# A second set of source rows, scaled from the first one layer later, and a reordered load queue, in a four-layer graph network

## The chip, the cores and the metric

The kernel runs on one core of a Trainium2 chip. The metric is device time in microseconds (us) of one execution, lower is better. The core has five instruction queues that run side by side and meet only at semaphores: PE (matmul), DVE (vector), ACT (activation functions, here mostly "scale and shift one tile of rows"), POOL (here: indirect gathers and scatters) and SP (here: nothing but issuing DMAs). Each queue runs its instructions in the order in which they are written; an instruction that waits on a semaphore holds all that stand behind it in its own queue.

## The reference, cut to what matters

50,000 nodes with 128 features, 12,500 edges sorted by target. Four layers, numbered 0 to 3 as in the code, each with a layer norm over the features after it:

```python
x = layernorm(x + L0(x, edges))      # attention over incoming edges
x = layernorm(x + L1(x, edges))      # mean of the neighbours, two products, relu
x = layernorm(x + L2(x, edges))      # per relation (8) product, summed over incoming edges
x = layernorm(x + L3(x, edges))      # messages by edge type (3), update by node type (3)

# layernorm(x) = (x - mean) / sqrt(var + 1e-5)

def L2(h, weight, src, dst, rel):
    hw = einsum('ni,rio->nro', h, weight)
    return segment_sum(hw[src, rel], dst)
def L3(h, W_e, b_e, W_n, b_n, src, dst, etype, ntype):
    parts = [relu(h)]
    for t in range(3):
        msg = where(etype == t, relu(h[src] @ W_e[t].T + b_e[t]), 0)
        parts.append(segment_sum(msg, dst))
    agg = concatenate(parts)
    return where_by_type(ntype, [agg @ W_n[t].T + b_n[t] for t in range(3)]) + h
```

A node without incoming edges gets zero from layer 2. For such a node the layer norm after layer 2 is only a second layer norm of what layer 1 left.

## The kernel before

Two kinds of rows are worked on. A **dense block** is 500 nodes (125 partitions x 4); there are 100 of them, and each goes through the layers as if it had no edges. An **edge chunk** is 500 edges; there are 25, and each layer runs over all of them, with one dense block (two in layer 0) threaded through each round. The rows of the source and the target node of every edge are kept apart in DRAM, as `source_rows` (`s_rows[0..2]`, one for the input of layers 1 to 3) and `target_rows` (`d_rows[0..2]`). In each layer a chunk's source rows are loaded by SP, and POOL then overwrites those whose node has incoming edges with the node's updated row, gathered from `target_rows` at `slot_all`.

Layer 1 makes two sets of source rows at once. ACT normalizes `ys` (a row plus its update) with the factors of statistics group "first" into `so`, the rows for layer 2, and again with those of group "third" into `so3`, the rows for layer 3 of a node that layer 2 leaves alone. Both have the same mean; their variances differ by the two lines in `variances` (L740, L743). SP stores both in `store_sources1` (L349, L351).

A round of layer 2 (loop variable c) on each queue, in the order of the code:

- DVE: `scan` of chunk c (L807), five of the seven relation masks of chunk c+1 (`masks`, L937, one product of `rel == r` and the chunk's rows per relation), the dense block (`read`, `stats`), the chunk's target rows (L946), variances, the first two masks of chunk c+2 (`EARLY = 2`), and then `scales`, whose last instruction (L757) releases ACT by `s_ln`. `masks` waits for the relation numbers of its chunk (`rl`).
- ACT: after `s_ln` of round c two sets of dense rows (L1039), the turned rows (L1076), the source rows of chunk c+3 (`evacuate_sources`, L1105), L1082, the target rows into `do`, and the dense block's result into `res`. So ACT's round c runs beside DVE's round c+1.
- PE: turns of rows (L1575, L1312), the eight relation products of chunk c+1 (L1561) in two halves with the turn of chunk c+2 between them, and the dense products (L1318, L1323, L1383).
- POOL: four gathers for chunk c+3 (L528), three lookups of node types.
- SP, one list of DMAs per round: load a dense block (L236), the source rows of chunk c+4 (`sources2`, L398), the relation numbers of chunk c+2 (`relations2`, L403), target rows (L413), `same` (L420), then wait for `do` of round c-1 and store it (`store2`, L426), then store a dense result (L242).

Layer 3 starts when POOL has seen every store of layer 2's target rows land (`landed(3)`) and gathers its first chunk. SP issues seven pairs of its first loads (L467 to L485) before the last `store2`. Layer 1 starts the same way behind layer 0.

Of the kernel before, what the change touches and what calls it, by code (L numbers as in the profile page):

```python
# [13 lines left out]
D = 128  # L14
# [33 lines left out]
def gnn_kernel(nc, x, src, dst, srcP, dstP, nextP, eattrT, etype3, etype8, eweight, ntype3, ntypeP, Wq, Wk, Wv, We, gate,  # L48
# [25 lines left out]
    with ctx:  # L74
# [6 lines left out]
        def two(make, name, *a):  # L81
# [53 lines left out]
        rel = two(sb, "rel", [D, C], I32)  # L135
        run, run2 = sb("run", [D, 3, C + 1]), sb("run2", [D, 3, C + 1])
        masked = sb("masked", [D, REL, C])
        den = sb("den", [R, T * H])
        headsel = sb("headsel", [D, H])
# [34 lines left out]
        SINGLE = ("tS tD eS eD eL pA pB pR vA vE vL eX eR nS nD nF yb eN sc", "tS tD eS eD pR vA nS nD rd",  # L174
                  "tS eS pM pR vA vM nD nF", "tS tD eS eD pM pR vM vA eX vN nD rd bs xb")
        RINGS = ({"aux": 2, "g": 3, "stS": 2, "stD": 2},
# [7 lines left out]
        s_slot = [sem(f"layer1_slots_{i}") for i in range(EC - SOONER + 1)]  # L184
# [28 lines left out]
        def _(sp):  # L213
# [145 lines left out]
            store_sources0(EC - 1)  # L359
# [17 lines left out]
            for c in range(EC):  # L377
                d = block_of(1, c)
                load_dense(d + 3)
                if there(c + 3):  # L380
                    rows1(c + 3)
                if there(c + 2):
                    targets1(c + 2)
                    sums1(c + 2)
                if c >= 1:
                    store_sources1(c - 1)
                    store_targets1(c - 1)
                    store_dense(d - 7)
# [39 lines left out]
            sources2(0)  # L428
            relations2(0)
            sources2(1)  # L430
            relations2(1)
            sums2(0)
            targets2(0)
            sums2(1)
            sources2(2)
# [5 lines left out]
            stored(1)  # L441
            sources2(3)
            for c in range(EC):
                d = block_of(2, c)
                if d + 3 < NC:
                    load_dense(d + 3)
                if there(c + 4):
                    sources2(c + 4)
                if there(c + 2):
                    relations2(c + 2)  # L450
                if there(c + 1):
                    targets2(c + 1)
                if there(c + 2):
                    sums2(c + 2)
                if c >= 1:
                    store2(c - 1)
                store_dense(d - 7)

            def sources3(c):
                k, q = c % 3, ph[3]  # L460
                sp.wait_ge(q["tS"], at(c - 2))
                if c == 0:
                    sp.wait_ge(ph[1]["rd"], EC)
                elif c < 3:
                    sp.wait_ge(ph[2]["tS"], EC - 3 + c)
                for part in PARTS:
                    sp.dma_start(flat(xs3[k])[part, :], rows(s_rows[2])[c][part, :]).then_inc(q["ld"][k], 16)  # L467
# [10 lines left out]
            def sums3(c):  # L478
                b, q = c % 2, ph[3]
                sp.wait_ge(q["vA"], at((c - 1) * NT))  # L480
                if c < 2:
                    sp.wait_ge(ph[2]["vA"], EC - c)
                    sp.wait_ge(ph[2]["vM"], (EC - c) * (REL - 1))
                sp.dma_start(same[b][:, :], to_all(same_d, c)).then_inc(q["sm"][b], 16)
                sp.dma_start(rel[b][:, :], to_all(etype3, c)).then_inc(q["sm"][b], 16)  # L485
# [32 lines left out]
        def _(pool):  # L518
# [75 lines left out]

            def rows1(c):
                k, q = c % 4, ph[1]
                pool.wait_ge(s_slot[max(c + 1 - SOONER, 0)], 16 * T * (SOONER if c < SOONER else 1))
# [9 lines left out]
            for c in range(EC):  # L607
# [3 lines left out]
                if c % 3 == 0 and there(late):  # L611
                    slots1(late * T, (late + 1) * T, s_slot[1 + c // 3])
# [45 lines left out]
        def _(dve):  # L658
# [8 lines left out]
            for k in range(3):  # L667
                V.memset(bst[k][:, :, :], 0.0)
            V.memset(floors[:, 0:1], D * EPS * EPS)
# [242 lines left out]

            step(V.memset(run[:, 0, C:C + 1], 0.0))
            source_sums1(0)
            for c in range(EC - 1):
# [7 lines left out]
                scales(s, 6, s_ln)  # L923
            step(edge_rows1(EC - 1, TAIL, 0, 1, 2))
            variances(TAIL, 3, 1)
            scales(TAIL, 3, s_tail)
            for d in range(block_of(1, EC - 1), block_of(1, EC) + GAP):
# [50 lines left out]
            def message_sums(c):  # L978
# [4 lines left out]
                for t in range(NT):  # L983
                    dve.wait_ge(q["eX"], c * NT + (t + 1))
                    V.scalar_tensor_tensor(out=masked[:, t, :], in0=rel[b][:, :], scalar=float(t), in1=masked[:, t, :],
                                           op0=ALU.is_equal, op1=ALU.mult).then_inc(q["vM"], 1)
                for t in range(NT):
                    dve.wait_ge(q["vM"], c * NT + (t + 1))
                    scan(m, t, same[b][:, :], masked[:, t, :], ALU.mult, ALU.add,
# [42 lines left out]
        def _(act):  # L1032
# [157 lines left out]
            for c in range(EC - 1):  # L1190
# [12 lines left out]
                act.wait_ge(q["stS"][b], (c // 2) * 2 * ROWS)  # L1203
                normalize(so[b], ys[b], k % 2, 4)
                normalize(so3[b], ys[b], k % 2, 1).then_inc(q["nS"], 1)
# [12 lines left out]
            act.wait_ge(q["stS"][b], ((EC - 1) // 2) * 2 * ROWS)  # L1218
            normalize(so[b], ys[b], TAIL, 1)
            normalize(so3[b], ys[b], TAIL, 0).then_inc(q["nS"], 1)  # L1220
# [3 lines left out]

            evacuate_sources(0, 2, 7)
# [6 lines left out]
            for c in range(EC - 1):  # L1232
# [11 lines left out]
                evacuate_xt(d - 1)  # L1244
                act.wait_ge(q["stD"][b], (c // 2) * ROWS)
# [420 lines left out]
```

## Time and profile before

| | |
|---|---|
| median of 3 runs | 1717.78 us (1715.58 to 1718.99) |
| the profiled execution | 1722.77 us, of which its span is 1721.0 us |
| busy over the span | PE 81%, DVE 82%, ACT 65%, POOL 71% |
| layer 0, with start and end | about 0 to 670 us |
| layer 1 | about 670 to 970 us |
| layer 2 | about 970 to 1350 us |
| layer 3 | about 1350 to 1721 us |

The busy shares are means over four layers that have different limits; a single layer has to be read from its own stretch. Times in a trace row are us from the start of the span. An engine's row gives its start, its length, the engine, the line of the kernel, the operation, the tile written and the tile read, the shapes, the count of instructions that the row stands for, and in brackets the idle time before it with what ended it.

### The profile page before, as it was taken

What the parts mean: (1) busy time and instruction counts of PE and PEld (TensorE: products, weight loads), DVE (VectorE), ACT (ScalarE), POOL (GpSimd) and SP (SyncE); (2) the same over time, 40 slices, a digit from 0 to 9 for tenths busy, and PEclk for the clock granted to TensorE, in tenths of its full rate; (3) what the DMA queues carried; (4) which work ended last, traced back from release to release, by engine and by line L of the source; (5) the groups of instructions that cost most, each with busy time, mean ns of one, the idle gap of its engine ahead of it and who ended that gap; (6) DMA issues with size and microseconds to landing.
All of it is one profiled execution on the core that took longest, in us unless ns stands there. A gap on an engine that the chain in (4) does not pass through costs nothing.

```text
span 1721.0 us, 22842 instructions
## 1 busy us (share of the span) xinstructions
PE 1390.8 (81%) x6078; PEld 902.0 (52%) x6078; DVE 1410.1 (82%) x3005; ACT 1120.2 (65%) x2769; POOL 1230.3 (71%) x910
## 2 busy tenths in 40 slices
PE   4687777777777755787878589999998699999995
PEld 2454444544445434666666355555555355555552
DVE  4688888888888874998889679999998578877774
ACT  1567877778777783999999836666665344334442
POOL 7877777777788877778888387776330668888874
PEclk9678999999999987989999889999999899999998
DMA  7334444444434343677777535555543434333320
GB/s 169 85 68 101 112 98 98 105 104 112 99 98 108 82 130 73 187 201 192 197 196 194 161 87 144 150 141 137 148 119 94 99 94 101 99 94 93 98 74 22
DMA packets 165796, 205.06 MB, mean 119 GB/s; under 512 B 66825, under 2 KB 97920, under 8 KB 165668
## 3 DMA queue, kind: packets, MB, share of 16 engines
q1 hardware_dynamic: 108068, 179.45, 38.8%
q0 software_dynamic: 57600, 24.15, 8.0%
q8 instruction: 50, 0.82, 0.2%
q14 instruction: 78, 0.64, 0.2%
HBM read 147.12 MB, written 70.80 MB: 127 GB/s over the span
## 4 chain that ended last, share of the span: by engine, by line
PE 48%; DVE 16%; ACT 12%; issue 12%; POOL 9%; DMA 2%; SPq 1%; POOLq 0%; DVEq 0%; ACTq 0%
PE po L1323 22%; PE pt L1312 6%; POOL slot_all L528 6%; DVE masked L937 5%; DVE bst L732 4%; ACT x L1039 3%; PE pb L1329 2%; PE pb L1561 2%; PE po L1318 2%; PE po L1383 2%; PE pc L1431 2%; ACT so L1039 2%; PE pc L1312 2%; ACT do L1039 2%; ACT res L1039 1%
## 5 line engine op out<-in xcount | busy, mean ns | idle before, releaser
L528 POOL DMA_INDIRECT xs<-target_rows,slot_all x236 | 316.9, 1343 | 160.9 <-issue 68.8
L1039 ACT ACTIVATE x<-y,nmr,rst 125x128 f32<-125x128 f32 x800 | 322.3, 480 | 43.2 <-DVE nmr L757 43.2
L1323 PE MATMUL po<-wnt,rt 128*125 128x384 f32 x800 | 290.1, 508 | 0.0
L1312 PE MATMUL pt<-ident,x 125*128 125x125 f32 x800 | 134.6, 295 | 111.2 <-issue 82.3
L1323 PEld LDWEIGHTS po<-wnt,rt 128*125 128x125 f32 x800 | 158.3, 201 | 92.3 <-issue 14.4
L1323 PE MATMUL po<-wnt,run 128*125 128x384 f32 x600 | 201.5, 486 | 0.0
L535 POOL DMA_INDIRECT out_rows<-do,last_all x100 | 146.6, 1466 | 60.7 <-issue 40.0
L528 POOL DMA_INDIRECT xs<-in_x,src_all x100 | 133.8, 1338 | 53.7 <-issue 53.7
L1312 PEld LDWEIGHTS pt<-ident,x 125*128 125x128 f32 x800 | 100.1, 154 | 136.9 <-issue 100.9
L1039 ACT ACTIVATE do<-yd,nmr,rst 125x128 f32<-125x128 f32 x400 | 163.5, 482 | 6.2 <-DVE nmr L757 6.2
L1039 ACT ACTIVATE res<-sel,nmr,rst 125x128 f32<-125x128 f32 x400 | 163.5, 482 | 3.8 <-DVE nmr L757 2.6
L528 POOL DMA_INDIRECT slot_all<-slot_d,src_all x100 | 136.3, 1363 | 34.2 <-issue 33.9
L528 POOL DMA_INDIRECT ntd_all<-in_ntype,dst_all x100 | 138.2, 1382 | 30.5 <-issue 30.2
L535 POOL DMA_INDIRECT slot_d<-eid,last_all x100 | 134.6, 1346 | 30.5 <-issue 30.2
L1561 PE MATMUL pb<-masked,wr 128*128 128x500 f32 x350 | 155.8, 586 | 0.0
L732 DVE BATCH_NORM_STATS2 bst<-y 125x6 f32<-125x256 f32 x400 | 142.9, 419 | 3.8
L1323 PEld LDWEIGHTS po<-wnt,run 128*125 128x125 f32 x600 | 108.8, 188 | 68.3
L528 POOL DMA_INDIRECT xdb<-target_rows,slot_all x64 | 84.6, 1321 | 83.7 <-DMA target_rows<-do 61.1
L1318 PE MATMUL po<-ball,ones_bf 128*125 128x384 bf16 x412 | 97.5, 365 | 46.0 <-DVE sel L778 46.0
L1105 ACT ACTIVATE st<-pt 128x500 f32<-128x500 f32 x50 | 29.0, 579 | 148.4 <-PE pt L1312 148.4
L937 DVE SCALAR_TENSOR_TENSOR masked<-rel,st 128x500 f32<-128x500 int32 x175 | 106.8, 669 | 10.8 <-issue 4.3
L1383 PEld LDWEIGHTS po<-wab,xt 128*125 128x125 f32 x800 | 102.7, 190 | 20.0 <-issue 0.2
(186 smaller groups left out, 3024.5 us busy)
## 6 DMA issues: line engine op xcount, KB each, us to landing
xin<-in_x SPq DMA_DIRECT2D x100, 224.0 KB
out_rows<-res SPq DMA_DIRECT2D x100, 224.0 KB
same<-same_d SPq DMA_DIRECT2D x75, 250.0 KB, 4.1
source_rows<-so SPq DMA_DIRECT2D x75, 224.0 KB
target_rows<-do SPq DMA_DIRECT2D x75, 224.0 KB
xs<-source_rows SPq DMA_DIRECT2D x59, 224.0 KB
rel<-in_etype SPq DMA_DIRECT2D x50, 250.0 KB, 4.8
xd<-target_rows SPq DMA_DIRECT2D x46, 224.0 KB
```

Of the source, the lines that this page charges most:

```text
L528: return nc.gpsimd.indirect_dma_start(out=to, out_offset=None, in_=table, in_offset=bass.IndirectOffsetOnAxis(ap=index, axis=0), bounds_ch ...
L535: return nc.gpsimd.indirect_dma_start(out=table, out_offset=bass.IndirectOffsetOnAxis(ap=index, axis=0), in_=of, in_offset=None, bounds_ch ...
L732: last = V.bn_stats(to, y[:, j:j + 2, :].rearrange("p j d -> p d j"))
L937: V.scalar_tensor_tensor(out=masked[:, r, :], in0=rel[b][:, :], scalar=float(r), in1=st[:, :], op0=ALU.is_equal, op1=ALU.mult).then_inc(q[ ...
L1039: last = A(to[:, j, :], y[:, j, :], ACT.Identity, scale=rst[s][:, k:k + 1], bias=nmr[s][:, k:k + 1])
L1312: last = nc.tensor.transpose(tile_of(to, j), rows_[:, j, :], ident[0:R, 0:R])
L1318: mm(po[0:R, j * 512:j * 512 + NT * D], ones_bf[:, 0:R], ball[:, :, :].rearrange("k s d -> k (s d)"), start=True, stop=False, skip_group_c ...
L1323: last = mm(po[0:R, j * 512:j * 512 + NT * D], left(j), wnt[:, k, :, :].rearrange("k t d -> k (t d)"), start=start, stop=stop, skip_group_ ...
L1329: last = mm(to[0:R, j * D:(j + 1) * D], left(j), right, start=start and j == 0, stop=stop and j == T - 1, skip_group_check=True)
L1383: last = mm(po[0:R, j * 512 + NT * D:(j + 1) * 512], xt[:, j, :], wab[:, 0, :], start=False, stop=True, skip_group_check=True)
L1431: mm(pc[:, 0:C], ks[:, :], st[:, :], start=False, stop=False)
L1561: mm(pb[:, 0:C], wr[:, r, :], masked[:, r, :] if r else st[:, :], start=r == 0, stop=r == REL - 1).then_inc(q["pM"], 1)
```

## The change

`so3` and its store leave layer 1. DVE computes there one factor per row instead (`factors1`, two small instructions per chunk, kept in `again_all`). In layer 2 ACT multiplies the rows of `xs2` by that factor (`source_rows2`, four instructions per chunk), and SP stores them (`store_sources2`). `sources2` also waits for that read. Layer 3 uses buffers of its own for two inputs (`aux` for `same`, `rel3` for `rel`), so that its first loads need not wait for layer 2's masks. SP's order changes: the first loads of layers 2 and 3 move into the last round of the layer before, those of layer 1 ahead of three stores. The semaphores for late `slot_all` lookups become a ring of three.

```diff
@@ stored(p)
-                    if p < 2:
-                        sp.wait_ge(ph[p]["stS"][b], (1 + p) * ROWS * n)
+                    sp.wait_ge(ph[p]["stS"][b], ROWS * n)
                     sp.wait_ge(ph[p]["stD"][b], ROWS * n)
@@ store_sources1(c)
-                for part in PARTS:
-                    sp.dma_start(rows(s_rows[2])[c][part, :], flat(so3[b])[part, :]).then_inc(q["stS"][b], 16)
@@ SP, start of layer 1
-            store_sources0(EC - 1)
             ...
             rows1(1)
             sums1(1)
+            rows1(2)
+            targets1(1)
+            store_sources0(EC - 1)
             store_targets0(EC - 2)
-            rows1(2)
             store_targets0(EC - 1)
-            targets1(1)
@@ sources2(c)
                 sp.wait_ge(q["tS"], at(c - 2))
-                sp.wait_ge(o["stS"][c % 2], counted(c, 2 * ROWS))
+                sp.wait_ge(q["nS"], at(c - 2))
+                sp.wait_ge(o["stS"][c % 2], counted(c, ROWS))
@@ new on SP
+            def store_sources2(c):
+                b, q = c % 2, ph[2]
+                sp.wait_ge(q["nS"], c + 1)
+                for part in PARTS:
+                    sp.dma_start(rows(s_rows[2])[c][part, :], flat(so3[b])[part, :]).then_inc(q["stS"][b], 16)
@@ SP, layer 1's loop
                     sums1(c + 2)
+                if c == EC - 1:
+                    sources2(0)
+                    relations2(0)
+                    sources2(1)
+                    relations2(1)
+                    sums2(0)
+                    targets2(0)
+                    sums2(1)
+                    sources2(2)
                 if c >= 1:
                     store_sources1(c - 1)
...
             stored(1)
+            store_sources2(0)
             sources2(3)
+            store_sources2(1)
@@ SP, layer 2's loop
                 if there(c + 2):
                     sums2(c + 2)
+                if c == EC - 1:
+                    sources3(0)
+                    targets3(0)
+                    sums3(0)
+                    sources3(1)
+                    sums3(1)
+                    sources3(2)
                 if c >= 1:
                     store2(c - 1)
+                if there(c + 2):
+                    store_sources2(c + 2)
                 store_dense(d - 7)
...
-            sources3(0)
-            targets3(0)
-            sums3(0)
-            sources3(1)
             targets3(1)
-            sums3(1)
-            sources3(2)
             store2(EC - 1)
@@ new on DVE, called after scales in each round of layer 1
+            def factors1(c, s, third, first):
+
+                of = lambda a, g: a[s][:, g * T:(g + 1) * T]
+                step(V.scalar_tensor_tensor(out=of(tmp, 0), in0=of(ve, first), scalar=1.0 / D, in1=of(rst, first), op0=ALU.mult, op1=ALU.mult))
+                V.tensor_tensor(again_all[:, c, :], of(tmp, 0), of(rst, third), ALU.mult).then_inc(ph[1]["vF"], 1)
@@ ACT, layer 1's loop
-                normalize(so[b], ys[b], k % 2, 4)
-                normalize(so3[b], ys[b], k % 2, 1).then_inc(q["nS"], 1)
+                normalize(so[b], ys[b], k % 2, 4).then_inc(q["nS"], 1)
@@ new on ACT
+            def source_rows2(c):
+                b, q = c % 2, ph[2]
+                act.wait_ge(q["stS"][b], (c // 2) * ROWS)
+                for j in range(T):
+                    last = A(so3[b][:, j, :], xs2[c % 3][:, j, :], ACT.Identity, scale=again_all[:, c, j:j + 1], bias=none[:, 0:1])
+                last.then_inc(q["nS"], 1)
+
             evacuate_sources(0, 2, 7)
+            act.wait_ge(ph[1]["vF"], EC)
+            source_rows2(0)
             act.wait_ge(ph[2]["vM"], REL - 1)
             evacuate_sources(1, 2, 7)
+            source_rows2(1)
@@ ACT, layer 2's loop
                     evacuate_sources(c + 3, 2, 7)
                 evacuate_xt(d - 1)
+                if there(c + 2):
+                    source_rows2(c + 2)
                 act.wait_ge(q["stD"][b], (c // 2) * ROWS)
                 normalize(do[b], yd[b], k % 2, 3).then_inc(q["nD"], 1)
@@ POOL, late lookups of slot_all
-                    slots1(late * T, (late + 1) * T, s_slot[1 + c // 3])
+                    k, n = slot_ring(late)
+                    pool.wait_ge(s_slot[k], 16 * T * (n - 1))
+                    slots1(late * T, (late + 1) * T, s_slot[k])
```

## Rows read from the trace of the kernel before

**Rows 1.** Windows, layers 1 and 2: us; busy PE, PEld, DVE, ACT, POOL; PE clock; DMA.

```profile
670.00:960.00 290.00, 231.68 (x1459) 189.68 (x1457) 261.12 (x623) 270.45 (x696) 234.59 (x173) 0.93 0.70 185
1024.00:1285.00 261.00, 256.19 (x1043) 154.06 (x1042) 255.53 (x559) 166.28 (x420) 160.17 (x120) 1.00 0.51 137
```

**Rows 2.** Waits in layer 1 (690 to 960 and 940): us, times, longest.

```profile
DVE tmp L754 <- ACT seed L1048: 18.1, 22, 1.4
POOL xs L528 <- DMA xs<-source_rows: 2.6, 2, 1.3
```

**Rows 3.** Timeline of ACT in one round of layer 1: both normalizations.

```profile
711.63 3.17 ACT L1039 ACTIVATE so<-ys,nmr,rst 125x128 f32<-125x128 f32 x8
```

**Rows 4.** Timeline of DVE, one small instruction on four columns.

```profile
1327.98 0.16 DVE L756 SCALAR_TENSOR_TENSOR rst<-tmp,seed 125x4 f32<-125x4 f32 x1
```

**Rows 5.** Timeline of SP in one round of layer 2.

```profile
1102.12 0.35 SPq L403 DMA_DIRECT2D rel<-in_etype  x1
...
1111.13 0.75 SPq L426 DMA_DIRECT2D target_rows<-do  x2
1112.67 0.77 SPq L242 DMA_DIRECT2D out_rows<-res  x2
...
1115.22 0.35 SPq L403 DMA_DIRECT2D rel<-in_etype  x1
```

**Rows 6.** Waits of SP in layer 2 (1024 to 1285): us, times, longest.

```profile
SPq L426 <- ACT do L1039: 144.7, 20, 7.8
```

**Rows 7.** Tile rel, layer 2 (1024 to 1285): issue to landing of 20 loads.

```profile
DMA to landing us min/median/max: 3.9/4.7/5.7
```

**Rows 8.** Timeline of DVE in the same round of layer 2.

```profile
1102.19 1.26 DVE L807 TENSOR_TENSOR_SCAN run<-same,run,pb 128x500 f32<-128x500 f32 x1
...
1113.35 1.26 DVE L937 SCALAR_TENSOR_TENSOR masked<-rel,st 128x500 f32<-128x500 int32 x2
...
1115.29 1.26 DVE L807 TENSOR_TENSOR_SCAN run<-same,run,pb 128x500 f32<-128x500 f32 x1
```

**Rows 9.** Timeline of ACT in the same round of layer 2.

```profile
1109.47 1.64 ACT L1039 ACTIVATE do<-yd,nmr,rst 125x128 f32<-125x128 f32 x4
1111.00 1.64 ACT L1039 ACTIVATE res<-sel,nmr,rst 125x128 f32<-125x128 f32 x4
```

**Rows 10.** Timeline of PE, same round: first turn, turn of chunk c+2, end.

```profile
1103.50 0.70 PE L1575 MATMUL pa<-ident,run 128*125 128x128 f32 x4 [0.25 <-DVE run L807]
1107.83 0.59 PE L1312 MATMUL pc<-ident,xs 125*128 125x125 f32 x4
1115.27 1.04 PE L1383 MATMUL po<-wab,xt 128*125 128x128 f32 x8
```

**Rows 11.** Window of 4 us in layer 2's first round: the PE clock.

```profile
1010.00:1014.00 4.00, 3.93 (x11) 2.86 (x12) 4.00 (x8) 0.59 (x1) 3.10 (x3) 0.50 0.83 238
```

**Rows 12.** Timeline of PE where it resumes after standing idle.

```profile
1010.07 1.21 PE L1575 MATMUL pa<-ident,run 128*125 128x128 f32 x4 [3.21 <-DVE run L807]
1017.22 0.59 PE L1312 MATMUL pc<-ident,xs 125*128 125x125 f32 x4
...
1330.45 1.54 PE L1318 MATMUL po<-ball,ones_bf 128*125 128x384 bf16 x4 [6.92 <-DVE sel L778]
1331.78 3.49 PE L1323 MATMUL po<-wnt,rt 128*125 128x384 f32 x8
1338.21 2.74 PE L1323 MATMUL po<-wnt,rt 128*125 128x384 f32 x8
```

**Rows 13.** Timeline of SP, ACT, POOL around the start of layer 3.

```profile
1328.37 1.65 ACT L1039 ACTIVATE do<-yd,nmr,rst 125x128 f32<-125x128 f32 x4 [0.82 <-DVE nmr L757]
1335.27 0.85 SPq L426 DMA_DIRECT2D target_rows<-do  x2
1342.71 1.27 POOL L528 DMA_INDIRECT xdb<-target_rows,slot_all  x1 [61.10 <-DMA target_rows<-do]
1351.74 0.59 ACT L1105 ACTIVATE st<-pt 128x500 f32<-128x500 f32 x1 [4.52 <-PE pt L1312]
```

More of the change, by code:

```diff
@@ L134, in gnn_kernel @@
         aux = two(sb, "aux", [D, C])
-        rel = two(sb, "rel", [D, C], I32)
+        rel, rel3 = two(sb, "rel", [D, C], I32), two(sb, "rel3_", [D, C], I32)
         run, run2 = sb("run", [D, 3, C + 1]), sb("run2", [D, 3, C + 1])
@@ L182, in gnn_kernel @@
                **{k: [sem(f"layer{n}_{k}_{i}") for i in range(ring)] for k, ring in RINGS[n].items()}} for n in range(4)]
-        s_slot = [sem(f"layer1_slots_{i}") for i in range(EC - SOONER + 1)]
+        s_slot = [sem(f"layer1_slots_{i}") for i in range(1 + 3)]
         s_types = sem("s_types")
@@ L376, in _ @@
             stored(0)
[L377 to L388, printed above, removed]
             def sources2(c):
@@ L426, in store2 @@
                     sp.dma_start(rows(d_rows[2])[c][part, :], flat(do[b])[part, :]).then_inc(q["stD"][b], 16)
[L428 to L435, printed above, removed]
+            for c in range(EC):
+                d = block_of(1, c)
+                load_dense(d + 3)
+                if there(c + 3):
+                    rows1(c + 3)
+                if there(c + 2):
+                    targets1(c + 2)
+                    sums1(c + 2)
+                if c == EC - 1:
[7 more added lines that the diff above has]
+                    sources2(2)
+                if c >= 1:
+                    store_sources1(c - 1)
+                    store_targets1(c - 1)
+                    store_dense(d - 7)
             store_targets1(EC - 1)
@@ L441, in _ @@
             stored(1)
+            store_sources2(0)
             sources2(3)
[L443 to L457, printed above, removed]
+            store_sources2(1)
             def sources3(c):
@@ L461, in sources3 @@
                 sp.wait_ge(q["tS"], at(c - 2))
+                sp.wait_ge(ph[2]["stS"][c % 2], counted(c, ROWS))
                 if c == 0:
@@ L481, in sums3 @@
                 if c < 2:
[L482 to L485, printed above, removed]
-            sources3(0)
-            targets3(0)
-            sums3(0)
-            sources3(1)
+                    sp.wait_ge(ph[1]["vA"], EC)
+                sp.dma_start(aux[b][:, :], to_all(same_d, c)).then_inc(q["sm"][b], 16)
+                sp.dma_start(rel3[b][:, :], to_all(etype3, c)).then_inc(q["sm"][b], 16)
+            for c in range(EC):
+                d = block_of(2, c)
+                if d + 3 < NC:
+                    load_dense(d + 3)
+                if there(c + 4):
+                    sources2(c + 4)
+                if there(c + 2):
+                    relations2(c + 2)
+                if there(c + 1):
+                    targets2(c + 1)
+                if there(c + 2):
+                    sums2(c + 2)
+                if c == EC - 1:
[5 more added lines that the diff above has]
+                    sources3(2)
+                if c >= 1:
+                    store2(c - 1)
+                if there(c + 2):
+                    store_sources2(c + 2)
+                store_dense(d - 7)
             targets3(1)
-            sums3(1)
-            sources3(2)
             store2(EC - 1)
@@ L593, in _, with slot_ring @@
             slots1(MARKS * (EC - MARKED), SOONER * T, s_slot[0])
+            def slot_ring(c):
+                return 1 + (c - SOONER) % 3, (c - SOONER) // 3 + 1
             def rows1(c):
                 k, q = c % 4, ph[1]
-                pool.wait_ge(s_slot[max(c + 1 - SOONER, 0)], 16 * T * (SOONER if c < SOONER else 1))
+                if c < SOONER:
+                    pool.wait_ge(s_slot[0], 16 * T * SOONER)
+                else:
+                    i, n = slot_ring(c)
+                    pool.wait_ge(s_slot[i], 16 * T * n)
                 pool.wait_ge(q["ld"][k], counted(c, ROWS, 4))
@@ L668, in _ @@
                 V.memset(bst[k][:, :, :], 0.0)
+            V.memset(none[:, :], 0.0)
             V.memset(floors[:, 0:1], D * EPS * EPS)
@@ L923, in _ @@
                 scales(s, 6, s_ln)
+                factors1(c, s, 1, 4)
             step(edge_rows1(EC - 1, TAIL, 0, 1, 2))
@@ L984, in message_sums @@
                     dve.wait_ge(q["eX"], c * NT + (t + 1))
-                    V.scalar_tensor_tensor(out=masked[:, t, :], in0=rel[b][:, :], scalar=float(t), in1=masked[:, t, :],
+                    V.scalar_tensor_tensor(out=masked[:, t, :], in0=rel3[b][:, :], scalar=float(t), in1=masked[:, t, :],
                                            op0=ALU.is_equal, op1=ALU.mult).then_inc(q["vM"], 1)
@@ L988, in message_sums @@
                     dve.wait_ge(q["vM"], c * NT + (t + 1))
-                    scan(m, t, same[b][:, :], masked[:, t, :], ALU.mult, ALU.add,
+                    scan(m, t, aux[b][:, :], masked[:, t, :], ALU.mult, ALU.add,
                          before[:, t, C:C + 1]).then_inc(q["vA"], 1)
@@ L1244, in _ @@
                 evacuate_xt(d - 1)
+                if there(c + 2):
+                    source_rows2(c + 2)
                 act.wait_ge(q["stD"][b], (c // 2) * ROWS)
```

14 lines of the change are left out of this document (8 added, 6 removed), and 2 rows, old and new, of the table RINGS.

## The prediction

> **What bounds the kernel now.** I read the windows by stage first, then for each layer the waits of its busiest engine, then the timelines of single rounds. In layer 1 ACT is busy 270.5 of 290 us and DVE 261.1 [rows 1]. DVE's only regular wait is for the seeds that ACT makes, 18.1 us in 22 rounds [rows 2]: ACT makes them behind the two normalizations of source rows (3.17 us for eight instructions [rows 3]), so there ACT sets the round and DVE is 0.8 us behind it. In layer 2 DVE is busy 255.5 of 261 us and PE 256.2, with PE at its full clock, 1.00 of 2.4 GHz, while ACT has 95 us to spare [rows 1]. A round is what lies between two scans, 1115.29 - 1102.19 = 13.10 us [rows 8]. SP stands most of each round at one place, the wait for `do` (144.7 us in 20 rounds [rows 6]), and issues nothing meanwhile: in the round shown there is no issue between the burst that holds the relation load at 1102.12 and the store at 1111.13 [rows 5]. What is written behind that wait goes out in one burst after it. Layer 3 starts late because its first gather waits for the last target rows to land [rows 13].
>
> **Layer 1: the second normalization goes.** Four of eight instructions, half of 3.17 us, so 1.6 us per round [rows 3]. DVE gets two small instructions of 0.16 us, 0.3 us [rows 4]. ACT's round falls below DVE's, so the round can gain what DVE waits today less the factors: 18.1/22 - 0.3 = 0.5 us, 12 us over 24 rounds, the upper end. The lower end is POOL: its 173 gathers and lookups fill 234.6 us with about 0.3 us of issue before each [rows 1], some 286 of 290 us, and its waits for loads are only 2.6 us [rows 2]. If POOL binds at once, 3 us are left. I take 8, the middle, with the two normalizations less in the layer's last rounds inside it.
>
> **Layer 2: where the new rows stand.** `source_rows2` is four ACT instructions just ahead of `do`; ACT has room for them, and that they cost 1.5 us of ACT hides behind DVE and PE. The cost is in the queue of SP. Today SP in its round c waits for `do` of ACT's round c-1. `store_sources2(c + 2)` in SP's round c waits for `nS` to reach c+3; two counts are given ahead of the loop and one in each round, so that count comes from ACT's round c itself: SP is held back one whole round. Behind the wait are the dense store and all loads of the next round, among them `relations2(c + 3)`. Those numbers are needed by DVE near the end of round c+1 (the two early masks), ahead of `scales`; `scales` starts ACT's round c+1, whose `source_rows2` frees SP for the load after. Nothing runs ahead any more; the chain closes once per round and its length becomes the round. The other late transfers have slack left: source rows are loaded four chunks ahead, dense blocks three, the target rows and `same` one to two.
>
> The length, counted from a scan as zero (1102.19 [rows 8]): the new rows take the place in which `do` stands now, and `do` ends where `res` can start, at 1111.0 to 1111.1 [rows 9]; SP's issue follows at 1111.13 [rows 5], so 8.9 us. The new store pair takes 0.8 us (as the pair of 0.77 does), and from the dense store to the relation load are 1115.22 - 1112.67 = 2.55 us [rows 5]: the load goes out at 12.3. It lands 4.7 us later [rows 7], at 17.0. From the first early mask to the next scan are 1115.29 - 1113.35 = 1.94 us [rows 8]. Together 18.9 us, against 13.1: 5.8 us more. Or from the other side: the mask starts at 11.2 today, the load would have to go out at 6.5 and goes out at 12.3.
>
> **What that does to PE.** PE now ends its round 14.1 us after the scan (1115.27 + 1.04 [rows 10]) and resumes 1.3 us after the next (1103.50 [rows 10]), so it would stand idle about 6 us in every round, where it stands 0.25 us today. After an idle stretch it was slow in this trace: in layer 2's first round it had stood 3.21 us [rows 12], and the next 4 us ran at 0.50 of full speed, the 1.2 GHz level [rows 11]. From its first turn to the turn of chunk c+2 took 1017.22 - 1010.07 = 7.15 us there [rows 12] against 1107.83 - 1103.50 = 4.33 at full clock [rows 10]: 2.8 us lost. That very piece lies on the chain, since ACT's rows of chunk c+3, which stand ahead of `source_rows2`, wait for that turn. After a stand of 6.92 us the products that followed took 3.49 us instead of 2.74 [rows 12]; with the slower bias products ahead of them I put the loss there at 1.4, an estimate. For a stand of 6 us I take 2.2, between the two, nearer to the row with the same instructions; the bounds are 0 and 2.8. The round is then 21.1 us, 8.0 more than today.
>
> The Trainium skill, TensorE: Matmul & The Clock Gate, section "HAM oscillation", says that a loop which leaves the array idle on a wait in each round finds it at half clock in each round again. It would give 21.1 us a round; the row after 3.21 us agrees, and no run here shows yet that it comes back in every round. A clock that stayed up would give 18.9.
>
> The relation loads of chunks 3 to 24 are late, 22 rounds. The first has no long stand of PE before it: 5.8 + 21 x 8.0 = 174 us.
>
> **Layer 3's start and the rest.** Seven pairs of loads no longer stand ahead of the last `store2`. Its rows are ready at 1330.0 (1328.37 + 1.65) and it goes out at 1335.27 [rows 13], 5.2 us late. The gather moves up by as much, but ACT, which takes the first turned rows, has only 4.5 us of idle time before them [rows 13]: gain 4.5, bounds 0 and 5.2. The loads of layer 2 that are issued sooner gain nothing by themselves, as PE comes to layer 2 behind its dense blocks; the ring of three semaphores waits for lookups nine rounds old; the loads of layer 1 ahead of stores leave layer 0's order alone, and its first gather waits for lookups on POOL: these edits I count as nothing, at most 2 us either way, and they are hidden by that PE and POOL work.
>
> **The sum.** +174 - 8 - 4.5 = +161 us. The profiled execution took 1722.77 us for a span of 1721.0, 5 us above the median of the runs; differences carry over, so from 1717.8 to 1879 us.
>
> **The rivals.** (1) The same chain with PE at full clock: 22 x 5.8 = 128, less 12.5, +115 us: 1833. For it: 6 us of stand are not sure to bring the slow level to this piece, and a busy PE came back quickly. Against: every long stand that I read was followed by slow products. (2) The chain does not close, and the relation numbers land in time: only the gains stay, -12.5 us: 1705. It decides at 6.5 us after the scan: if SP passes the store's wait before that, no mask is late. For it, today's slack of 6 us; against, `do` ends at 8.9 and the new rows can't end sooner in the same place. This is the case on the other side. (3) PE stays at half clock through the round: 12.8 us of work become about 25.6, and the round some 26.5; 22 x 13.4 less 12.5 is +280: 2000. Against: in layer 2's first round the clock came back after some 5 us. (4) The moved loads and the missing store change nothing, as POOL and DVE bind in layer 1: the gains fall to 3 and the forecast rises to 1888; that is inside its range.
>
> **How the numbers follow.** The forecast has 0.65 (with rival 4 in it), rival 1 0.20, rival 2 0.07, rival 3 0.04, and 0.04 is left for what I have not seen, half of it near no change. With landings of 3.9 to 5.7 us and losses of 0 to 2.8 the round lies between 18.1 and 22.7, so the time between 1815 and 1920; I give 1822 to 1915, which holds most of the forecast and of rival 1. About 0.2% either way is what a measurement of this kernel can tell from no change: faster 0.07, same 0.02, slower 0.91.
>
> **What would show it.** In the changed profile layer 2's rounds should be 19 to 22 us long; DVE's first early mask should wait about 6 to 8 us per round for the DMA of `rel`; SP should wait at `store_sources2` for ACT, and the relation load should go out some 12 us or more after the scan; PE should stand 6 us per round, with a granted clock under 0.9. DVE's wait for seeds in layer 1 should be gone and its rounds 11.6 to 12 us. Layer 3's first gather should follow its last store without seven loads ahead. If the masks don't wait, the step that counts SP's rounds is wrong, and with it the whole forecast; if they wait and PE is never slow, the clock's term is.

## The result and the profile after

The changed kernel takes 1880.85 us (median of 4 runs, 1877.66 to 1883.86), the kernel before 1718.38 us beside it: a ratio of 1.0947, 95% interval 1.092 to 1.0974, or 162.5 us more. The forecast was 1879 us.

The windows of the changed kernel, layer 1 and layer 2, in the columns of [rows 1]:

```profile
670.00:930.00 260.00, 210.12 (x1376) 170.65 (x1375) 251.38 (x636) 228.91 (x582) 211.81 (x159) 0.98 0.67 178
1020.00:1470.00 450.00, 315.63 (x1093) 190.56 (x1092) 267.52 (x582) 203.27 (x521) 158.89 (x114) 0.82 0.34 95
```

In layer 1 ACT falls from 93% to 88% of the window and DVE rises from 90% to 97%. Layer 2 is where the time went. Its DVE and PE, both at 98% in [rows 1], fall to 59% and 70%; PE's clock falls from 1.00 to 0.82, and DMA from 137 to 95 GB/s. No engine and no queue is full: something waits in a ring.

The waits of DVE in layer 2 of the changed kernel (1000 to 1480; us, times, longest) name one end of that ring:

```profile
DVE masked L965 <- DMA rel<-in_etype: 176.7, 21, 9.9
```

And those of SP in the same stretch name the other:

```profile
SPq L411 <- ACT so L1255: 358.5, 23, 18.2
```

The early masks wait 8.4 us for the relation load in each of 21 rounds; the kernel before has no such wait. SP stands at `store_sources2` (L411) for 358.5 us, 15.6 a round, where it stood 7.2 a round at `store2` (144.7 / 20 [rows 6]).

The chain of waits through one round of layer 2 (start, us, what), from one early mask to the next:

```profile
1189.69 1.28 DVE masked L965 x2
...
1191.62 1.27 DVE run L827
...
1192.93 1.21 PE pa L1613 x4
...
1200.07 0.59 ACT st L1133
...
1201.13 1.53 ACT so L1255 x4
...
1202.68 0.30 SPq L411
...
1203.48 0.34 SPq L243
...
1204.34 0.36 SPq L237
...
1205.27 0.31 SPq L383
...
1206.07 4.95 DMA rel<-in_etype
...
1211.09 1.28 DVE masked L965 x2
...
1213.02 1.27 DVE run L827
```

Read it as a ring: the scan (1191.62), PE's turns and products, ACT's source rows of chunk c+3 (`st`), ACT's new rows (`so`), SP's store of them (L411) that waited for these rows and the three pairs that stand between it and the relation load, the load itself, the mask, the next scan. That is 21.40 us, against 13.10 between the scans of [rows 8]; from scan 1038.97 to scan 1467.24 the 20 rounds have a mean of 21.41.

Where the time of the whole went, from the scans of the two traces:

| stretch | before | after | difference |
|---|---|---|---|
| first to last scan of layer 1 | 287.5 | 274.3 | -13.2 |
| to the first scan of layer 2 | 54.4 | 50.4 | -4.1 |
| first to last scan of layer 2 | 312.3 | 495.7 | +183.4 |
| to the first mask of layer 3 | 34.2 | 31.8 | -2.4 |

The sum is +163.7 us, the runs say +162.5. Two more stretches: what follows is 0.7 us shorter, and what precedes (layer 0) was 8.1 us shorter in this one execution, the first scan of layer 1 standing at 658.69 instead of 666.79. With them the two profiled executions differ by 154.9 us, less than the medians: that of the kernel before (1722.77) lies 4.4 us above its median, the changed one (1877.66) 3.2 below. The last two stretches are not counted to the change (experiment 8 says what speaks for that).

### The profile page after: what moved, and what is told of

The parts are those of the page before. It is cut to its first block, busy times and chain, and to the rows that moved or that the text cites. A ratio compares the mean times of both kernels' runs of the same rounds, so it can differ in the third digit from the quotient of the medians.

```text
span 1875.9 us, 22922 instructions
## 1 busy us (share of the span) xinstructions
PE 1420.8 (76%) x6078; PEld 918.3 (49%) x6078; DVE 1416.2 (75%) x3056; ACT 1120.2 (60%) x2769; POOL 1240.0 (66%) x910
## 4 chain that ended last, share of the span: by engine, by line
PE 45%; ACT 15%; issue 12%; POOL 11%; DMA 7%; DVE 6%; SPq 3%; POOLq 0%; DVEq 0%; ACTq 0%
PE po L1361 18%; PE pb L1599 7%; POOL slot_all L537 6%; DMA rel<-in_etype 6%; PE pt L1350 5%; ACT x L1067 3%; POOL xs L537 2%; ACT so L1255 2%; DVE run L827 2%; ACT so L1067 2%; ACT do L1067 2%; DVE masked L965 2%; PE pa L1613 2%; PE pc L1350 1%; PE pb L1367 1%
## 5 line engine op out<-in xcount | busy, mean ns | idle before, releaser
L1361 PE MATMUL po<-wnt,rt 128*125 128x384 f32 x800 | 279.2, 493 | 0.0
L1350 PE MATMUL pt<-ident,x 125*128 125x125 f32 x800 | 144.1, 311 | 82.0 <-issue 60.3
L1361 PEld LDWEIGHTS po<-wnt,rt 128*125 128x125 f32 x800 | 151.0, 192 | 86.2 <-issue 4.5
L1599 PE MATMUL pb<-masked,wr 128*128 128x500 f32 x350 | 168.0, 624 | 0.0
L537 POOL DMA_INDIRECT xs<-in_x,src_all x100 | 139.0, 1390 | 38.0 <-issue 38.0
L1350 PEld LDWEIGHTS pt<-ident,x 125*128 125x128 f32 x800 | 109.4, 164 | 107.0 <-issue 80.8
L544 POOL DMA_INDIRECT slot_d<-eid,last_all x100 | 127.0, 1270 | 30.5 <-issue 30.2
L1613 PE MATMUL pa<-ident,run 128*125 128x128 f32 x100 | 28.6, 437 | 144.1 <-DVE run L827 144.1
L1356 PE MATMUL po<-ball,ones_bf 128*125 128x384 bf16 x412 | 90.4, 344 | 48.3 <-DVE sel L798 48.3
L1599 PEld LDWEIGHTS pb<-masked,wr 128*128 128x128 f32 x350 | 73.5, 215 | 89.5 <-issue 76.7
```

The lines of the kernel that those rows point to most:

```text
L537: return nc.gpsimd.indirect_dma_start(out=to, out_offset=None, in_=table, in_offset=bass.IndirectOffsetOnAxis(ap=index, axis=0), bounds_ch ...
L544: return nc.gpsimd.indirect_dma_start(out=table, out_offset=bass.IndirectOffsetOnAxis(ap=index, axis=0), in_=of, in_offset=None, bounds_ch ...
L1350: last = nc.tensor.transpose(tile_of(to, j), rows_[:, j, :], ident[0:R, 0:R])
L1356: mm(po[0:R, j * 512:j * 512 + NT * D], ones_bf[:, 0:R], ball[:, :, :].rearrange("k s d -> k (s d)"), start=True, stop=False, skip_group_c ...
L1361: last = mm(po[0:R, j * 512:j * 512 + NT * D], left(j), wnt[:, k, :, :].rearrange("k t d -> k (t d)"), start=start, stop=stop, skip_group_ ...
L1599: mm(pb[:, 0:C], wr[:, r, :], masked[:, r, :] if r else st[:, :], start=r == 0, stop=r == REL - 1).then_inc(q["pM"], 1)
```

## The experiments

The **theory** is the forecast's: the relation load stands in SP's list behind a wait for ACT's own round, so that the ring closes, and 2.2 us of the ring are PE at half clock. **Rival 1**: what holds the round are the other late loads, above all the source rows, for which POOL waits longer than DVE does for the relation numbers (1000 to 1480):

```profile
POOL xs L537 <- DMA xs<-source_rows: 221.2, 19, 15.7
```

**Rival 2**: the four ACT instructions and the store cost the time where they stand, whatever the order. For the clock the rival is that the slow stretch has another cause. Each ratio below is to the kernel before, run beside that experiment (medians of 1718 to 1722 us).

**1. Only the relation load moved.**

```diff
@@ layer 2, SP's round c
-                if there(c + 2):
-                    relations2(c + 2)          # relations2(2) goes ahead of the loop
...
                 if c >= 1:
                     store2(c - 1)
+                if there(c + 3):
+                    relations2(c + 3)
                 if there(c + 2):
                     store_sources2(c + 2)
```

> The changed kernel, with one load moved: in layer 2 the relation load of chunk c+3 is issued in round c just ahead of the wait of the new store; the store, its wait and all other loads stay. Theory (the relation load behind that wait is the only thing that closes the chain): no mask waits for it any more, layer 2's round falls from 21.4 to 13.1 us and the time to 1718 less 13 (layer 1) less 2.4 (start of layer 3), about 1703 us (1690 to 1712). Rival 1 (the round is held by the other late loads, above all the source rows for which POOL waits 230 us): the round stays above 18 us and the time above 1810. Rival 2 (the new rows on ACT and their stores cost the time by themselves): 1880 stays.

1702.31 us, ratio 0.9886 (0.9861 to 0.9911): 1.1% faster than the kernel before, and faster than the changed one. One load of 250 KB, at another place in the list, is worth some 178 us. Layer 2's window in this kernel:

```profile
1020.00:1290.00 270.00, 263.52 (x1065) 157.63 (x1064) 262.92 (x573) 199.24 (x511) 157.62 (x117) 1.00 0.56 156
```

SP and DVE in one round, from the timeline of the same kernel:

```profile
1105.33 0.75 SPq L411 DMA_DIRECT2D source_rows<-so  x2
...
1110.94 0.37 SPq L388 DMA_DIRECT2D rel<-in_etype  x1
...
1118.44 0.75 SPq L411 DMA_DIRECT2D source_rows<-so  x2
...
1120.64 1.26 DVE L966 SCALAR_TENSOR_TENSOR masked<-rel,st 128x500 f32<-128x500 int32 x2
```

And the waits of SP and POOL in its layer 2 (1000 to 1300):

```profile
SPq L411 <- ACT so L1256: 162.9, 21, 18.9
POOL xs L538 <- DMA xs<-source_rows: 71.6, 19, 11.1
```

The load now leaves at 1110.94, 9.70 us ahead of the mask that reads it (1120.64), which waits for nothing. SP still stands at the new store for 7.8 us a round, and all other loads stay late with it: that costs nothing. PE is at 1.00 throughout, and the round is 13.13 us (mean of 21). The rows, their ACT time and their stores are all still there, so rival 2 is out; the source rows and every other load still leave behind ACT's round, and POOL still waits 3.8 us for source rows in each of 19 rounds, so rival 1 is out.

**2. The store one round later, nothing else.**

```diff
-            store_sources2(1)                  # ahead of the loop
...
-                if there(c + 2):
-                    store_sources2(c + 2)
+                if there(c + 1):
+                    store_sources2(c + 1)
```

> The changed kernel, with the new store written one round later in SP's list (chunk c+1 in round c), so that its own wait is for ACT's round before. Theory: nothing is freed, since the source-row load of chunk c+4, which stands ahead of the relation load, waits for the same count of ACT; the chain stays closed, and only becomes shorter by the store pair, the dense store and the dense load, that now go out before the wait: 2.9 us of some 3.7 (1118.34 - 1115.43), so 22 x 2.9 = 64 us, 1817 us (1795 to 1835). A reader who holds the store's wait alone for the cause expects 1703. Rival 2 (cost of the rows and transfers themselves): 1880.

1811.42 us, ratio 1.0531 (1.0505 to 1.0557). The wait of its DVE in layer 2 (1020 to 1390):

```profile
DVE masked L964 <- DMA rel<-in_etype: 102.5, 19, 6.6
```

And that of its SP:

```profile
SPq L379 <- ACT so L1254: 232.0, 19, 13.8
```

SP no longer stands at the store but at `sources2` (L379), which the change made wait for the same count of ACT. The ring is as closed as it was, 18.55 us long in the 19 rounds 2 to 20 (counted from 0, as `c`). From round 21 on there are no source rows left to load, and with them the ring goes: the next two rounds take 14.80 and 13.12 us. Whoever had looked at the store alone would have mended the wrong line: the change put two waits for ACT's round ahead of the relation load, and either is enough (experiment 4 shows the store's wait alone).

**3. The store one round later, and the relation load first in SP's round.**

```diff
 (as 2, and)
+                if there(c + 2):
+                    relations2(c + 2)
                 if d + 3 < NC:
                     load_dense(d + 3)
                 if there(c + 4):
                     sources2(c + 4)
-                if there(c + 2):
-                    relations2(c + 2)
```

> The changed kernel with the store one round later and the relation load first in SP's round, ahead of the dense load and of the source-row load that waits for ACT. Theory: both waits now stand behind the relation load, the chain is open, 13.1 us a round and 1703 us (1690 to 1712). Rival 1 (the late source rows): above 1810. Rival 2: 1880.

1701.89 us, ratio 0.9898 (0.9868 to 0.9927). Both waits stand behind the load now; ten rounds take 131.5 us (scans 1016.30 to 1147.77). Together, 2 and 3 show that the ring needs both: the wait, and the load behind it.

**4. A smaller dose: the load first in the round, as in 3, the store and its wait as in the change.**

> The changed kernel with the relation load first in SP's round, still behind the new store's wait: a smaller dose. Theory: the load goes out 2.05 us sooner (1118.34 - 1116.29), the chain is shorter by that and the round 19.4 us; 22 x 2.05 = 45 us, 1836 us (1815 to 1845). Rivals 1 and 2: no change, 1880.

1856.51 us, ratio 1.0784 (1.0755 to 1.0813): the direction is the theory's, the size is 24 us where 45 were expected, outside the expected range. In the chain of this kernel the load follows two pairs behind the wait:

```profile
1213.97 0.30 SPq L411
...
1214.31 0.40 SPq L411
...
1214.76 0.34 SPq L243
...
1215.14 0.41 SPq L243
...
1215.59 5.95 DMA rel<-in_etype
```

The mean round is 20.23 us, 1.18 less than 21.41. From the end of ACT's rows to the load it is 1.70 us instead of 3.15, a gain of 1.45 and not 2.05: in the changed kernel's last rounds there are no dense or source loads left to stand in between (1.67 us in the last two late rounds), so its mean was below the round that I had read. And the slow stretch of PE, from its first turn to `st`, is 7.47 us instead of 7.24. 21 rounds of 1.18 are 25 us.

**5 and 6. PE kept busy while it would stand.** Ahead of PE's wait for the scan, in rounds 1 to 22, products whose results nothing uses go into the bank that PE overwrites next (waiting first until DVE has read it).

```diff
+                if 1 <= c < EC - 2:
+                    pe.wait_ge(q["nF"], c)
+                    for r in range(14):          # 7 in the second run
+                        mm(pa[:, 0:C], wr[:, r % 4, :], wr[:, 0:4, :]...[:, 0:C], start=True, stop=True)
                 pe.wait_ge(q["vA"], c + 1)
```

> The changed kernel, order and waits untouched; in layer 2's rounds 1 to 22 PE does 14 further products of 128x500 into the bank that it overwrites next, while it would stand waiting for the scan (14 x 0.42 = 5.9 us at full clock, within the stand of 6.4). Their results are used by nothing. Theory of the forecast (2.2 us of each round are PE at half clock after its stand): from PE's first turn to the evacuated source rows falls from 7.24 to 5.0 us, the round from 21.4 to 19.2 and the time by 22 x 2.2 = 48 us, to 1833 (1825 to 1845). Rival (the stretch is slow for another reason, as waits for weights or for banks): 7.24 stays, and the time stays at 1880 or rises.

1952.77 us, ratio 1.136 (1.1327 to 1.1392): neither forecast. PE and DVE of the kernel with 14 products, from the timeline of one round:

```profile
1102.53 11.90 PE L1613 MATMUL pa<-wr 128*128 128x500 f32 x28
...
1108.32 1.26 DVE L827 TENSOR_TENSOR_SCAN run<-same,run,pb 128x500 f32<-128x500 f32 x1
...
1114.27 0.60 PE L1617 MATMUL pa<-ident,run 128*125 128x128 f32 x4
```

I had mis-sized the products: 14 count as 28 instructions and take 11.90 us, so PE takes up the scan of 1108.32 only at 1114.27, 4.6 us later than it could. But the stretch in question did become short, 4.91 us in place of 7.24 in all 19 rounds measured. Hence the second run with half of them.

> As the run before with products in PE's stand, but 7 products in place of 14: a product counts as two instructions of 0.42 us, so the 14 took 11.9 us and ran 4.8 us past the scan; 7 take 5.9 us, inside the stand of 6.4. Theory: first turn to evacuated rows 4.9 to 5.0 us in place of 7.24, the round 19.1 to 19.5 us, the time 22 x 2.0 to 2.2 less, 1835 us (1825 to 1848). Rival (the products cost as much as the clock gives back, or the stand was not what made PE slow): 1870 or more.

1842.97 us, ratio 1.0717 (1.0694 to 1.0741), 38 us less than the changed kernel. The window of layer 2 of the kernel with 7 products:

```profile
1020.00:1430.00 410.00, 391.86 (x1391) 214.70 (x1389) 270.44 (x589) 204.05 (x523) 163.43 (x117) 1.00 0.38 107
```

PE around one scan, from its timeline:

```profile
1104.19 0.70 PE L1617 MATMUL pa<-ident,run 128*125 128x128 f32 x4 [0.51 <-DVE run L827]
...
1116.83 6.03 PE L1613 MATMUL pa<-wr 128*128 128x500 f32 x14
```

The clock is 1.00 all through, the stretch from the first turn to `st` 5.00 us, the round 19.19 (rounds 2 to 22). More work on PE makes the kernel faster: the clock's term is real, 2.2 us per round, and the ring without it is what the forecast's first rival described.

**7. Where layer 1's gain comes from.** The next four start from the repaired kernel of experiment 1. Here the four ACT instructions return to layer 1, without the store.

```diff
                 normalize(so[b], ys[b], k % 2, 4).then_inc(q["nS"], 1)
+                normalize(so3[b], ys[b], k % 2, 1)
```

> The repaired kernel (relation load ahead of the wait, 1702 us) with the four ACT instructions that made the fourth layer's rows put back into layer 1's rounds; their store stays away and what they write is used by nothing. If layer 1's gain of 13 us comes from ACT: it is lost, 24 x 0.55, and the time is 1715 (1710 to 1719), layer 1's round 12.0 us. If it comes from the store pair that left the queues: 1702 stays.

1715.38 us, ratio 0.9976 (0.996 to 0.9991). Half of DVE's wait of [rows 2], of which neither the changed nor the repaired kernel has anything, is back (690 to 940):

```profile
DVE tmp L775 <- ACT seed L1077: 8.9, 19, 1.1
```

It is 0.4 us a round where it was 0.8; the factors, which stay on DVE here, take up 0.28 of the difference (experiment 10). First to last scan of layer 1 take 286.6 us (663.67 to 950.24) against 275.4 in experiment 1, and from there to layer 2's first scan 54.5 against 51.1. The gain is ACT's, in the layer and in the blocks behind it; the store pair that left the queues gave nothing that can be seen.

**8. SP's order between layers 0 and 1 as in the kernel before** (the last stores of layer 0 ahead of layer 1's first loads).

> The repaired kernel with SP's order between layer 0 and layer 1 as in the kernel before (the last stores of layer 0 ahead of the first loads of layer 1). If the loads moved ahead of stores gave the 8 us by which layer 1 begins sooner in the changed kernel's trace: 1710, first gather of layer 1 at about 657 us. If that is only how one execution of layer 0 differs from another: 1702 (1700 to 1705), first gather between 649 and 654 us as in the other traces.

1703.46 us, ratio 0.9908 (0.9887 to 0.993), beside 1703.7 for the kernel of experiment 11 on the same chip. The first scan of layer 1 stands at 663.61; in the eleven other traces whose layer 0 is the same it lies between 658.69 and 663.67. The moved loads gave nothing that the runs can show, and the old order does not bring back 666.79; so I take the 8 us for how one execution of layer 0 differs from another. Of the kernel before itself there is one trace, so how often it stands there is not known.

**9. Layer 3's first loads behind the loop again, ahead of the last `store2`.**

> The repaired kernel with the first loads of layer 3 issued behind layer 2's loop again, ahead of the last target store, as in the kernel before. By the forecast's term for layer 3's start it loses 4.5 us (1707); by the first reading of the changed kernel's trace 2.4 (1704.5); rival: the loads were hidden anyway, 1702.

1704.68 us, ratio 0.9925 (0.9902 to 0.9948): 0.4% above experiment 1 by the ratios, with intervals that overlap. The traces, one execution of each, are sharper. POOL's first gather and DVE's first mask of layer 3, from the timeline of the kernel with the loads behind:

```profile
1323.01 1.27 POOL L537 DMA_INDIRECT xdb<-target_rows,slot_all  x1 [50.21 <-DMA target_rows<-do]
...
1335.83 0.68 DVE L1013 SCALAR_TENSOR_TENSOR masked<-rel,masked 128x500 f32<-128x500 int32 x1 [9.32 <-ACT masked L1302]
```

The same two in the kernel of experiment 1:

```profile
1318.46 1.27 POOL L538 DMA_INDIRECT xdb<-target_rows,slot_all  x1 [43.08 <-DMA target_rows<-do]
...
1334.04 0.68 DVE L1014 SCALAR_TENSOR_TENSOR masked<-rel,masked 128x500 f32<-128x500 int32 x1 [4.82 <-ACT masked L1303]
```

From layer 2's last scan (1301.78 and 1304.35) the gather comes after 21.2 and 14.1 us, the mask after 34.1 and 29.7. The gather moves up 7.1 us, and 4.4 of them reach DVE. What stops the rest is told below, at the forecast's term for layer 3.

**10. Layer 1 without the factors** (`factors1` gone, all factors one, so the fourth layer's rows are not scaled).

> The repaired kernel without the factors of layer 1 (the two small DVE instructions of each chunk); the factors are all one, so the fourth layer's rows come out unscaled. If DVE sets layer 1's round now: 24 x 0.33 = 8 us less, 1694 (1690 to 1697). If POOL sets it: 1702 stays.

1692.41 us, ratio 0.9843 (0.9812 to 0.9874). First to last scan of layer 1 take 268.8 us (662.65 to 931.44), 6.6 less than in experiment 1: 0.28 us a round. So DVE sets layer 1's round in the repaired kernel, and POOL, whose seven gathers and lookups of 1.27 us and 0.30 of issue make 11.0 us, is just below the 11.2 that are left.

**11. Both repairs at once** (experiments 1 and 2 together).

> The changed kernel with both repairs: the relation load of chunk c+3 early in round c, and the new store one round later. Theory: the chain is already open with either, DVE and PE set layer 2's round, so nothing more is gained: 1702 us (1698 to 1705), a ratio of 0.990 to the kernel before.

1703.7 us (median of 6 runs), ratio 0.99 (0.9884 to 0.9917). Nothing more is gained: with the ring open, DVE and PE set the round.

## Why the prediction was right, point by point

The mechanism was the one forecast, and the total came out 2 us off. The steps of the ring, forecast and mean of 20 rounds of the changed kernel:

| step | forecast | measured |
|---|---|---|
| scan to end of ACT's new rows | 8.9 + 2.2 for the clock | 11.1 |
| to the relation load's issue | 3.4 | 3.15 |
| to the mask (landing) | 4.7 | 5.2 |
| mask to scan | 1.94 | 1.92 |
| round | 21.1 | 21.41 |

**SP's rounds.** The step on which everything hung, that the count for `store_sources2(c + 2)` comes from ACT's round c itself, is shown by the waits of SP and by experiments 1 and 3. The forecast missed that `sources2` waits for the same count: it named one wait where there are two (experiment 2), and the source rows, to which it gave slack, come late as well (POOL waits 221.2 us for them). For the time of this kernel that makes no difference, for the repair it decides.

**The landing** was taken from [rows 7], a median of 4.7 us. In the chain of the changed kernel 20 landings lie between 4.63 and 5.62, their mean is 5.1: the term was 0.4 us short. When the load is issued first behind its wait and the dense pairs are out already (experiment 2), 16 landings have a mean of 4.5. The Trainium skill, DMA: Bandwidth & Descriptors, section "Anatomy of one DMA — SWDGE (gpsimd) path", has for transfers that GpSimd issues a fixed 2.0 us and the bytes at 436 GB/s, by which these 250 KB are an estimate of 2.6 us. This load, issued by SP and spread from one row over 128 partitions, took twice that: the page's figure is for another path and does not carry over to it.

**PE's clock** was the term with the widest bounds, 0 to 2.8. The windows of PE in the round shown above:

```profile
1192.90:1194.90 2.00, 1.97 (x9) 1.97 (x10) 2.00 (x4) 0.47 (x2) 1.70 (x2) 0.50 0.05 7
1194.90:1196.90 2.00, 2.00 (x4) 0.89 (x4) 2.00 (x4) 1.89 (x5) 1.70 (x2) 0.50 0.05 8
1196.90:1198.90 2.00, 2.00 (x5) 0.76 (x4) 1.93 (x4) 0.23 (x1) 1.69 (x2) 0.91 0.15 10
1198.90:1200.90 2.00, 2.00 (x12) 1.39 (x11) 1.97 (x7) 0.83 (x2) 0.61 (x1) 1.00 0.07 1
```

After its stand of 6.4 us PE runs at 0.50, the 1.2 GHz level, for some 4 us and then comes back to 2.4 GHz. From the first turn to `st` are 7.24 us in the mean, 5.01 where the clock is 1.00 (experiment 1): 2.23 lost, 2.2 forecast. The Trainium skill, TensorE: Matmul & The Clock Gate, section "HAM oscillation — how this bites in real kernels", says that a loop which leaves the array idle on a wait in each round is slow in each round anew. This trace agrees, with 0.82 as the clock of the layer: what stood open in the forecast is settled in its favour.

That the term comes out to a tenth is luck. It leaned most on one row, the first round of layer 2 in the kernel before, and such a row is one draw: PE stands 3.21 us there in all thirteen traces, and its stretch from the first turn to `st` then takes 5.0 us in four of them (experiments 3, 6, 7 and 8), 6.7 in three and 7.8 to 8.0 in six, the kernel before among them. What held is that the slow stretch comes in every round of the ring: 6.44 to 8.05 us in all of rounds 2 to 22.

Rival 1 of the forecast (1833, that is +115) fails on this alone. Experiment 6 makes its condition true and comes to +121.7 beside its own kernel before. In its trace layer 2 is 140.4 us longer where rival 1 has 128: the rounds take 19.19 us for 18.9, and the first late one 25.15, as PE comes to its turn only 6.8 us after the scan, behind the unused products. Layer 1 and the blocks behind it give 7.3 us more than the forecast's 8, layer 3's start 2 less. Rival 2 (the chain does not close, 1705) is what the repaired kernel does, at 1702. Rival 3, half clock through the round, did not come: from 1198.90 on the clock is 1.00.

**Layer 2 in all**: 174 us forecast, 183.4 measured. 21 rounds at 21.41 instead of 13.01 (the mean before, 312.3 / 24) are 176.4; the other three rounds, the first late one among them, cost 7.0 where 5.8 stood. The steps of the round err in both directions: the issue came 0.25 us sooner, the landing 0.5 later.

**Layer 1** was mis-sized: 8 us with the blocks behind it, 13.2 and 4.1 measured, and rounds of 11.4 us where 11.6 to 12 were forecast. The step that failed is the lower bound by POOL, which pulled the value to the middle: POOL does not bind (experiment 10), and the upper bound, DVE's wait of 0.82 us per round less the factors, was the answer; the factors cost 0.28 us, as the 0.3 forecast. The stretch behind the layer, where ACT works on too, comes on top of it (experiment 7).

**Layer 3's start**: 4.5 forecast, 2.4 in the changed kernel, 4.4 between experiments 9 and 1. The gather moved up further than forecast, from 21.7 us after the last scan (the kernel before; 21.2 in experiment 9) to 14.1 in the changed and the repaired kernel. Less of it arrives for the forecast's own reason: ACT has only its idle time to give. In experiment 9 the first `st` of layer 3 waits for PE, which has waited 9.4 us for the gathered rows; in the changed kernel, where the gathered rows come sooner, it starts right behind the dense block's `res`, as it does in experiment 1:

```profile
1332.30 0.59 ACT L1133 ACTIVATE st<-pt 128x500 f32<-128x500 f32 x1 [4.25 <-PE pt L1350]
```

```profile
1505.82 1.65 ACT L1067 ACTIVATE res<-sel,nmr,rst 125x128 f32<-125x128 f32 x4 [0.87 <-DVE nmr L777]
1507.37 0.56 ACT L1133 ACTIVATE st<-pt 128x500 f32<-128x500 f32 x1
```

So the dense blocks set the first mask in these two kernels. It stands 29.7 to 32.0 us after the last scan in the eleven traces with the loads moved, against 34.2 and 34.0 in the two without. The changed kernel's is 2.1 us behind the repaired one's mostly because these blocks begin later: PE takes up the turn of the last scan only 1.7 us after that scan's end, behind dense products of the round before.

The errors were +9 in layer 2, -9 in layer 1 and behind it, +2 at layer 3: the forecast's 2 us are luck in part, and the bounds of its terms are the better measure of it.

## What to carry to other kernels

In a queue that only issues DMAs, a wait delays every load written behind it: before adding one, ask from which round of the other engine its count comes, and which load behind it is needed first. If that load's data lead back to the count, its slack does not shrink, it is gone, and the length of the ring becomes the round. Look then for every wait ahead of the load that the ring could close through (here two), and move the load rather than the wait.

## What the runs showed of the hardware that had not been expected

The half-clock stretch does not grow with the stand that precedes it: mean stands of 3.6 us (experiment 2), 5.0 (4) and 6.4 (the changed kernel) lost 2.1, 2.5 and 2.2 us against the 5.01 at full clock. From the changed kernel to experiment 2 the shorter ring so saved its own length and nothing of the clock; with a stand of 0.3 us (experiment 1) nothing is lost. The stretch differs from round to round, 6.44 to 8.05 us in the changed kernel, mostly in a sequence of three (about 8.0, 7.0 and 6.7), so the moment at which the clock returns moves against the round.

Nor does a stand of one length always bring the slow level. After 3.21 us PE's first turn of layer 2 took 1.21 us in the kernel before [rows 12]. In experiment 6, after the same stand and with no unused products ahead of it yet, it took 0.70:

```profile
989.28 0.70 PE L1617 MATMUL pa<-ident,run 128*125 128x128 f32 x4 [3.21 <-DVE run L827]
```

What decides between the two, no run here shows. A loss read from a single round of a trace is one of several possible values, and its mean over many rounds is the better price.
